# A bias row loaded once and spread by TensorE, in a sort-then-multiply kernel

## The reference

```
y[b] = x[b] + w[subject[b]]^T x[b] + bias[subject[b]]       # 64 x 64 weights, a bias per channel
z[b] = y[b] + y[b] W^T + s[k] (y[b] A[k]^T) Bm[k]^T         # k = adapter[b], 512 x 512 W, rank 16
```

## Time and profile before

| | us |
|---|---|
| median of 3 runs | 241.74 |
| lowest and highest | 240.59, 242.06 |
| the profiled execution | 241.67 |
| its span | 239.9 |
| PE busy | 228.6 (95% of the span) |
| DVE, ACT, POOL busy | 149.3, 108.0, 80.0 |
| granted PE clock, mean | 0.997 |

### The profile page before, as it was taken

How to read it: one execution, slowest core, us unless ns; L and a number is a source line. 1 busy time by engine, 2 the same in 40 slices (tenths; PEclk the granted TensorE clock), 3 DMA queues, 4 the chain that set the end, 5 groups by cost and what they waited for, 6 DMA issues and landing times.

```text
span 239.9 us, 9652 instructions
## 1 busy us (share of the span) xinstructions
PE 228.6 (95%) x2900; PEld 186.9 (78%) x2901; DVE 149.3 (62%) x259; ACT 108.0 (45%) x185; POOL 80.0 (33%) x277
## 2 busy tenths in 40 slices
PE   1798999999999999999999999999999999999993
PEld 1676888888888888888788888888888888888862
DVE  6798857775358735874358824875348755435753
ACT  2174573653435353563425445453426534353541
POOL 3468780710067620520046740535134141000000
PEclk9999999999999999999999999999999999999998
DMA  5956465735565474635645563655657364561333
GB/s 128 293 151 190 145 179 133 216 97 153 159 172 164 131 217 109 197 109 171 179 131 176 139 209 105 190 144 133 174 136 212 90 197 113 160 194 46 90 87 90
DMA packets 23723, 36.64 MB, mean 153 GB/s; under 512 B 6162, under 2 KB 6162, under 8 KB 23698
## 3 DMA queue, kind: packets, MB, share of 16 engines
q1 hardware_dynamic: 16640, 26.36, 40.5%
q10 hardware_dynamic: 7058, 9.97, 13.6%
HBM read 19.53 MB, written 16.78 MB: 151 GB/s over the span
## 4 chain that ended last, share of the span: by engine, by line
PE 88%; DVE 4%; DMA 2%; issue 2%; ACT 1%; ACTq 1%; POOL 0%; DVEq 0%; POOLq 0%
PE ps L901 69%; PE ps L861 14%; PE ps L837 3%; DMA x_ring<-in_x_dram 2%; DVE o_ring L558 1%; ACTq L709 1%; PE ps L793 1%; ACT x_hi L663 1%; ACT m_f L682 1%; PE ps L831 0%; DVE x_lo L538 0%; PE ps L889 0%; DVE last_parts L543 0%; PE ps L890 0%; PE ps L892 0%
## 5 line engine op out<-in xcount | busy, mean ns | idle before, releaser
L901 PE MATMUL ps<-m_hi,x_hi 128*128 x244 | 97.0, 398 | 0.0
L901 PE MATMUL ps<-m_hi,x_lo 128*128 x244 | 95.1, 390 | 0.0
L901 PE MATMUL ps<-m_lo,x_hi 128*128 x244 | 95.1, 390 | 0.0
L538 DVE TENSOR_TENSOR x_lo<-x,x_hi 128x512 fp32r<-128x512 f32 x64 | 44.4, 694 | 62.9 <-ACT x_hi L663 62.6
L374 POOL COPY p_pair<-p_all 64x64 f32 x128 | 44.6, 349 | 114.0 <-DVE x L530 96.8
L663 ACT ACTIVATE x_hi<-x 128x512 fp32r<-128x512 f32 x64 | 40.4, 632 | 55.3 <-ACT o_ring L676 30.0
L676 ACT ACTIVATE o_ring<-ps 128x512 f32<-128x512 f32 x60 | 35.9, 598 | 52.6 <-PE ps L901 51.3
L901 PEld LDWEIGHTS ps<-m_hi,x_hi 128*128 128x128 f32 x244 | 45.7, 187 | 10.7 <-issue 0.3
L901 PEld LDWEIGHTS ps<-m_hi,x_lo 128*128 128x128 f32 x244 | 45.8, 188 | 9.7
L901 PEld LDWEIGHTS ps<-m_lo,x_hi 128*128 128x128 f32 x244 | 45.8, 188 | 9.0
L530 DVE TENSOR_TENSOR x<-ps,bias_pair 128x512 f32<-128x512 f32 x64 | 43.6, 685 | 12.0 <-PE ps L861 10.8
(11 more groups left out here) (103 smaller groups left out, 79.7 us busy)
## 6 DMA issues: line engine op xcount, KB each, us to landing
x_ring<-in_x_dram SPq DMA_DIRECT2D x124, 128.0 KB, 2.7
out_dram<-o_ring ACTq DMA_DIRECT2D x64, 128.0 KB, 2.6
out_dram<-o_ring SPq DMA_DIRECT2D x64, 128.0 KB, 2.3
a_f<-in_L_cond_A_dram SPq DMA_DIRECT2D x8, 128.0 KB, 2.6
o_ring<-in_L_cond_W_dram SPq DMA_DIRECT2D x2, 256.0 KB, 4.7
o_ring<-in_L_cond_W_dram ACTq DMA_DIRECT2D x2, 256.0 KB, 6.0
x_ring<-in_x_dram ACTq DMA_DIRECT2D x4, 128.0 KB, 3.3
b_nat<-in_L_cond_Bm_dram ACTq DMA_DIRECT2D x1, 256.0 KB, 3.7
```

The costliest lines, as they stand in the source:

```text
L538: nc.vector.tensor_tensor(x1_lo[:, u % HELD], x1[:, u % 2], x1_hi[:, u % HELD], ALU.subtract).then_inc(x1_lo_ready, 1)
L901: mm = nc.tensor.matmul(ps[:, 2 + u % 2, :], part, m_tile(m, k, c), start=(c == 0 and part is hi and m is m_hi), stop=(c == TC - 1 and par ...
```

## The change

Five things are done together.

1. The bias is loaded once, as a row of 2 KB into partition 0 of `bias_row` (128 x 512), by ACT, as its second DMA instead of its last. DVE first sets `bias_row` to zero, as its first instruction, and ACT waits for that (`bias_zeroed`).
2. PE multiplies a 128 x 128 matrix of ones with `bias_row`, in four parts of 128 columns, into PSUM bank 0: two parts before the matmul of `order`, two after the tables of subjects and places. ACT copies the bank to `bias_all`, after its first two x loads. POOL waits for that copy (`bias_ready`) where it waited for the DMA. The counts of the sort move to bank 1.
3. W's block 0 is transposed before the matmul of `batch` instead of after the tables.
4. At step 2 PE waits ahead of its first layers for the parameters of three pairs (4 to 6); for those of pair 7 it waits just before pair 7's own.
5. Outside the loop the register of the second layer is read ahead of `quad_inputs` instead of behind it.

```diff
+        bias_row = sb("bias_row", [P, S * C])
@@ gpsimd, the first pair
-                    pool.wait_ge(bias_in, 16)
+                    pool.wait_ge(bias_ready, 1)
@@ vector
-            counts, earlier = ps[:, 0, 0:K], ps[:, 0, K:2 * K]
+            counts, earlier = ps[:, 1, 0:K], ps[:, 1, K:2 * K]
+            nc.vector.memset(bias_row[:], 0.0).then_inc(bias_zeroed, 1)
             dve.wait_ge(consts, 2)
@@ scalar
+            act.wait_ge(bias_zeroed, 1)
+            act.dma_start(bias_row[0:1, :], bias.rearrange("s d -> (s d)").rearrange("(a n) -> a n", a=1)).then_inc(bias_in, 16)
             act.dma_start(scal_row[:], scal.rearrange("(a k) -> a k", a=1)).then_inc(scal_in, 16)
@@ behind W's blocks 2 and 3
-            act.dma_start(bias_all[:], bias.rearrange("s d -> (s d)").rearrange("(a n) -> a n", a=1)
-                          .to_broadcast([P, S * C]).rearrange("p (s d) -> p s d", s=S)).then_inc(bias_in, 16)
@@ behind the first x loads of ACT
+            act.wait_ge(bias_spread, 1)
+            nc.scalar.activation(bias_all[:].rearrange("p s d -> p (s d)"), ps[:, 0, :], ACT.Copy).then_inc(bias_ready, 1)
             a_round(0, 0)
@@ tensor
+            def spread_bias(part):
+                cols = slice(part * P, part * P + P)
+                return nc.tensor.matmul(ps[:, 0, cols], ones[:], bias_row[:, cols], start=True, stop=True)
+            pe.wait_ge(bias_in, 16)
+            for part in range(2):
+                spread_bias(part)
             pe.wait_ge(firsts_ready, 1)
...
+            pe.wait_ge(w_in[0], 16)
+            for c in range(TC):
+                turn_w(0, c)
             pe.wait_ge(place_ready, 1)
...
-            pe.wait_ge(w_in[0], 16)
-            for c in range(TC):
-                turn_w(0, c)
+            for part in range(2, TC):
+                mm = spread_bias(part)
+            mm.then_inc(bias_spread, 1)
             turn_b(0)
@@ quad_inputs
-                pe.wait_ge(pair_ready, j * 4 + 4 * L0_QUAD)
+                pe.wait_ge(pair_ready, j * 4 + 4 * (L0_QUAD - (1 if isinstance(j, int) and j == XR else 0)))
@@ a step of TensorE
-                if l0_pairs:
+                if l0_pairs and n is not None:
                     quad_inputs(j + 2)
                 ... the register is read here
+                if l0_pairs and n is None:
+                    quad_inputs(j + 2)
                 for i in l0_pairs:
+                    if n is None and j == 2 and i == 5:
+                        pe.wait_ge(pair_ready, 4 * (XR + L0_QUAD))
                     layer0(j + i, u + i)
```

More of the change, by code:

```diff
@@ L149, in cond_residual_layers @@
         bias_in = sem("bias_in")
+        bias_zeroed = sem("bias_zeroed")
+        bias_spread = sem("bias_spread")
+        bias_ready = sem("bias_ready")
         bnat_in = sem("bnat_in")
@@ L777, in _ @@
             pe.wait_ge(oh_ready, 1)
-            nc.tensor.matmul(ps[:, 0, 0:K], ones_b[:], onehot[:], start=True, stop=True)
-            nc.tensor.matmul(ps[:, 0, K:2 * K], before_b[:], onehot[:], start=True, stop=True).then_inc(counted, 1)
+            nc.tensor.matmul(ps[:, 1, 0:K], ones_b[:], onehot[:], start=True, stop=True)
+            nc.tensor.matmul(ps[:, 1, K:2 * K], before_b[:], onehot[:], start=True, stop=True).then_inc(counted, 1)
             def turn_w(o, c):
```

## The result

The changed kernel is slower, not faster: 242.67 us median (241.86 to 243.57, 11 executions) against 241.27 for the kernel before (240.59 to 242.06, 11). The ratio is 1.0058 with a 95% interval of 1.0045 to 1.0070, so 1.4 us lost where I forecast 0.9 us gained. That is inside the forecast's 1% and outside its range, 239.8 to 241.9.

What follows compares the result with a forecast made beforehand. PE was taken as the bound from its first layer on. PE's sequence allowed 0.75 + 0.3 = 1.05 us, x only 0.9; the smaller gave 241.67 - 0.9 = 240.8 us, range 239.8 to 241.9.

Steps and rivals of the forecast that it cites:

- The failed step: ACT's queue: `b_nat` issued some 0.5 us later lands near 6.1 instead of 5.6, delaying `turn_b` by up to 0.5 us.
- The cover: Ahead of the A parts: DVE's 0.83 us wait for ACT hides `b_nat`'s delay of up to 0.5 us.
- The slower rival: Sort: PE stands before `firsts` until the bias row lands; 242.0 us, at the far end 245.5; 5%.
- The zeroing: Start of the sort: DVE's memset of the bias row moves DVE's sequence by +0.1 us, POOL's iota by nothing.
- the rival's 0.5 us: Prologue: a lock on the port shared by DVE and POOL delays POOL's iota, about 0.5 us worse, 241.3 us; 5%.
- The spread: Sort: the first two parts take 1.11 us on PE, from 3.5 to 4.6, hidden before `firsts` at 4.8.
- W's block 0 ahead of `place`: Sort: four transposes in front of the next matmul make `batch` 0.1 us late, bounds 0 and 0.4.
- The missing table: Prologue loads: 256 KB less gives x 1.05 us and `a_f` 0.5 us, bounds 0 and 1.05.
- my 0.3 us for that step: First layer: PE's gain there from `a_f` coming 0.5 us sooner, bounds -0.3 and 1.05.
- a sign: Prologue: POOL's first bias copy at about 9.8 us would show the forecast right.
- The hole: Step 2, at 21.95 us: PE's 0.75 us hole closes, unless x holds it.
- The sum: Step 2: 0.75 + 0.3 = 1.05 us by PE's sequence, 0.9 us by x; the smaller counts, 240.8 us.

Runs made afterwards that it cites:

- the hole alone: Kernel before with only the step 2 waits changed: three pairs' parameters first, pair 7's apart, register read ahead of the wait; 0.9973, 240.61 us.
- the run with the row: Changed kernel with `b_nat` second on SP, W's block 0 on ACT and its transposes behind the tables again; 0.9978, 240.78 us.
- the one with the table: Kernel before with only the step 2 waits changed, plus `b_nat` second on SP and W's block 0 on ACT; bias table kept, no spread; 0.9972, 240.54 us.
- the register read alone: Kernel before with only the register read moved ahead of the waits at step 2, still waiting for all four pairs' parameters; 0.9983, 240.85 us.
- by the row: Kernel before plus DVE's memset, ACT's wait for it and the unused bias row's DMA ahead of the scalings, table still loaded; 1.0068, 242.78 us.
- by the wait: Kernel before plus only a wait of ACT for POOL's constants ahead of the `b_nat` DMA; 1.0089, 243.22 us.
- the run with W's block 0 back: Changed kernel with the four transposes of W's block 0 moved back behind the tables, ahead of the spread's last two parts; 1.0047.
- the filled run: Changed kernel with three more float32 products of the spread, results unused, on PE ahead of `turn_b`; 1.0030, 241.91 us.
- the run with `b_nat` first: Changed kernel with ACT issuing `b_nat` ahead of its wait for the zeroed row and ahead of the bias row; 1.0047.

## Why the prediction was wrong

**The failed step** is the one on ACT's queue: "`b_nat` lands now at 5.6 (1.9 + 3.7) and then near 6.1". I had moved the landing by the 0.5 us of its issue. It moved by 1.65 in the changed kernel, and by 2.0 in the run where its issue moved by 0.3. I had counted what is issued in front of the moved DMA, and not SP's loads on the other queue, which now stood otherwise to it: a duration read in one order of transfers was used for another. With 7.24 in its place my own sum would have read: widening at 8.2, `turn_b` near 9.4, and ten transposes behind that, which is the chain of the profile after but for the slower widening.

**The cover.** I named DVE's 0.83 us as what hides up to 0.5. But behind `turn_b` stands PE's own queue, and its cover was PE's wait of 1.33 us for x ahead of the first layer. `turn_b` moved from 7.86 to 9.87, 2.0 us (1.6 by the start of the widening, 0.4 by its length), and the transposes behind it took 3.7 us instead of 3.0: 2.0 + 0.7 - 1.33 = 1.4 us, the 1.34 by which the first layer is late.

**The slower rival** was the right kind (PE waits for a DMA that moved) with the wrong DMA: here the row was there at 3.79. It became true once `b_nat` was put in front of it.

**The zeroing** cost nothing, below my 0.1: `onehot` still starts at 2.95 us, where the ids land. POOL's iota started at 0.95 and 1.14 as before with the memset beside it at 1.04 to 1.52. The Trainium skill's page "SBUF — State Buffer" ("SBUF: two separate sides") ties its exclusive lock to VectorE operations in a two-port mode or with two SBUF inputs. This memset and these POOL operations overlapped, so the rival's 0.5 us didn't arise.

**The spread** was 1.22 us for two parts (taken: 1.11) and hidden in the sort: the matmul of `order` started at 4.94 instead of 4.76, its copy on ACT at 5.50 instead of 5.45. **W's block 0 ahead of `place`** made `batch` 0.43 us late (6.91 against 6.48), the upper bound and not the 0.1 that I took: the next matmul came behind all four transposes, at 6.60, and not 0.3 us before their modelled end (6.67).

**The missing table.** `a_f` landed 2.4 us earlier (8.9 against 11.25), more than twice my upper bound of 1.05. Not all of that is the table's: with the same loads as before, `a_f` took 3.7 us instead of 4.9 in the profile of the hole alone, and landed at 10.0. And it was worth nothing: with everything else put right, the run with the row (0.9978) and the one with the table (0.9972) are equal. Where x and `a_f` were early, PE's own prologue was the next bound, and so my 0.3 us for that step falls. POOL's first bias copy came at 11.18 us, not at the 9.8 that I gave as a sign: ACT had the bias ready at 9.86, but POOL was late by its widening.

**The hole** was right in mechanism and size: forecast 0.75 or what x leaves of it, measured 0.65 us by the ratio (0.9973), in a kernel whose prologue is on time. The register read alone gave 0.4 of it; my split was 0.53 and 0.2.

**The sum, redone.** The two can't be added up as separate terms. `b_nat`'s lateness costs 1.6 us by the ratio (by the row) to 2.1 (by the wait) in kernels that keep the old waits, and their traces have no hole at step 2 either (0.00 and 0.03 us): a PE that comes late finds POOL done. So once `b_nat` was late, changes 4 and 5 had nothing left to give, and the changed kernel is about as slow as the one with the row. Why the one with the wait is slower still (1.0089, six executions) is open. In the profiled pair PE is 1.28 us late when the matmuls ahead of step 2 begin (22.77 against 21.49), and the closed hole, by whichever of the two, leaves 0.52 of it (23.22 against 22.70). From the first layers of step 2, by the timeline, to the end of the span all seventeen profiled executions take 216.8 to 217.5 us, so what an execution loses it loses before. The changed kernel's median execution has a span of 241.0 us; by that it reaches step 2 near 24.0 us, an estimate, 0.8 later than the profiled one.

**Pace, a part of that cost.** In the changed kernel's profile the bf16 products behind `turn_b` that add the identity (L840), each with two float32 transposes ahead of it, come 0.53 us apart up to 13.11, then 0.28 apart; in the kernel before the fast pace begins at 9.8. Changed kernel:

```profile
12.06 0.31 PE L840 MATMUL ps<-ident_b 128*128 128x128 bf16 x1
...
12.59 0.31 PE L840 MATMUL ps<-ident_b 128*128 128x128 bf16 x1
...
13.11 0.22 PE L840 MATMUL ps<-ident_b 128*128 128x128 bf16 x1
...
13.39 0.22 PE L840 MATMUL ps<-ident_b 128*128 128x128 bf16 x1
```

What it is worth is seen in the two kernels that only issue `b_nat` later. Their PE instructions are the same, and `turn_b` starts at 9.81 and 9.89. By the wait, fast from 13.05 (241.90 us), and by the row, slow up to the first layer (242.82 us):

```profile
13.48 0.69 PE L862 MATMUL ps<-p_pair,x_ring 64*64 64x64 f32 x32
...
23.19 2.10 PE L862 MATMUL ps<-p_pair,x_ring 64*64 64x64 f32 x128
```
```profile
13.92 1.03 PE L868 MATMUL ps<-p_pair,x_ring 64*64 64x64 f32 x32
...
23.93 2.09 PE L868 MATMUL ps<-p_pair,x_ring 64*64 64x64 f32 x128
```

That is 0.7 us at step 2. The pace doesn't follow the code alone: the kernel before, the register read alone and the hole alone are the same up to step 2, and their profiles are fast from 9.8, 10.0 and 11.5 us. In the run with W's block 0 back, whose profiled execution (242.70) is as long as the changed kernel's median, the slow pace lasts into the first M at 14.9. Each kernel has one trace, so that the pace makes the difference between executions of one kernel is not shown.

The granted clock reads 1.00 in both stretches, so here the column doesn't show it. PE had stood idle for 1.64 us just ahead of them, and the run that filled that time is 0.7 us faster. The Trainium skill, page "TensorE: Matmul & The Clock Gate", section "What's actually happening", says that the throttled clock is the default and sustained activity releases it; the filled run's time agrees in direction, its trace doesn't show an earlier rise.

**Open.** Why the landing of `b_nat` jumps: of the 1.7 us beyond its later issue, SP's loads are 1.1, and for the other 0.6 no run speaks. And how much of the 1.4 us is pace: no trace of a typical execution of the changed kernel is there.

## What to carry to other kernels

A DMA that is issued a few tenths later can land two microseconds later, so when an edit puts anything in front of a DMA, ask what the other queue transfers in that time, and price it from both. Before you pay for relieving a resource, ask what PE itself has queued in front of the same point; here 256 KB less brought nothing. Two changes that fill the same idle time of PE don't add up: the hole closed by itself when PE was late. Move register reads ahead of a wait: that was 0.4 us for one line.

## What the runs showed that I had not expected

- `b_nat`'s landing by its issue: 1.33 on SP, 4.1 to 4.3 us; 1.32 on ACT, 5.3 to 5.4; 1.89, 5.6; 2.20, 7.6; 2.34, 7.2 to 7.6. With SP's loads in another order: 2.21 with both behind it, 6.5; 2.35 with W's block 1 ahead of `p_all`, 6.8.
- After PE had stood idle for 2.0 us in the run with `b_nat` first, the granted clock of the next 3.5 us was 0.53, so at the 1.2 GHz level for most of it, and the first 512-column matmuls there came 0.43 us apart instead of 0.23. The windows of that run, from 15.9 to 24 us:

```profile
15.90:17.90 2.00, 0.05 (x4) 0.00 (x0) 2.00 (x5) 1.43 (x3) 0.80 (x5) 0.97 0.28 96
17.90:21.40 3.50, 3.48 (x38) 2.90 (x39) 2.02 (x5) 0.90 (x3) 2.81 (x12) 0.53 0.68 205
21.40:24.00 2.60, 2.60 (x13) 2.11 (x12) 2.57 (x4) 1.47 (x3) 1.57 (x4) 1.00 0.32 103
```

That execution took 244.74 us, 2.3 us over the median of its kernel.
